# Low-rank products added to the base weights once per batch, in a kernel of attention, low-rank feed-forward and routed experts

## The reference, cut to what matters

```python
y = einsum(x, weight[id]) + bias[id]                       # cond
Q, K, V = y @ W_Q, y @ W_K, y @ W_V                        # 16 heads of 16
x1 = x + softmax(causal(Q K^T / 4)) V @ W_o
hid = relu(x1 @ wi^T + 2*(x1 @ common_wi_a^T) @ common_wi_b^T + 2*(x1 @ Wa_i[id]^T) @ Wb_i[id]^T)
h = hid @ wo^T + 2*(hid @ common_wo_a^T) @ common_wo_b^T + 2*(hid @ Wa_o[id]^T) @ Wb_o[id]^T   # F = 1024, ranks 16 + 16
out = x1 + top2 of 8 experts(h), three dense layers 256-512-512-256 with gelu, weighted by the softmax gate
```

## Time and profile before

| what | value |
|---|---|
| median of 3 runs | 1477.07 us (1468.75 to 1480.15) |
| the profiled execution | 1473.53 us, its span 1471.8 us |
| mean granted PE clock | 0.94 |
| busy: PE, DVE, ACT, POOL | 1299.8, 814.7, 682.5, 515.0 us |

### The profile page before, as it was taken

How to read it: one execution, slowest core, us unless ns; L and a number is a source line. 1 busy time by engine, 2 the same in 40 slices (tenths; PEclk the granted TensorE clock), 3 DMA queues, 4 the chain that set the end, 5 groups by cost and what they waited for, 6 DMA issues and landing times.

```text
span 1471.8 us, 26713 instructions
## 1 busy us (share of the span) xinstructions
PE 1299.8 (88%) x8313; PEld 974.7 (66%) x8314; DVE 814.7 (55%) x1753; ACT 682.5 (46%) x1301; POOL 515.0 (35%) x809
## 2 busy tenths in 40 slices
PE   5878989988988988989989885459899999999997
PEld 3436656656656656656666554448788888888886
DVE  4626646646646646556556433745455555555553
ACT  4654654655655655655655630023333333333332
POOL 0332332332332432432332420324354444544442
PEclk9579999999999999999999978569999999999998
DMA  5112223222232132132132223733525224242220
GB/s 176 44 48 89 83 77 116 79 85 96 80 123 87 64 122 82 65 123 87 55 113 79 80 86 129 292 137 73 217 43 155 36 43 141 52 148 38 38 43 11
DMA packets 50765, 137.54 MB, mean 93 GB/s; under 512 B 10658, under 2 KB 29730, under 8 KB 49026
## 3 DMA queue, kind: packets, MB, share of 16 engines
q0 software_dynamic: 28992, 68.35, 16.4%
q1 hardware_dynamic: 21698, 68.18, 12.8%
HBM read 86.03 MB, written 51.38 MB: 93 GB/s over the span
## 4 chain that ended last, share of the span: by engine, by line
PE 71%; DVE 11%; ACT 8%; DMA 3%; issue 3%; POOL 3%; SPq 0%; POOLq 0%; DVEq 0%; ACTq 0%
PE bank L691 65%; PE bank L973 4%; DVE nmax L1359 4%; ACT q_sb L1160 3%; ACT probs_t L1153 2%; PE bank L965 1%; DVE hid_low L1286 1%; DMA xg<-hrows,gid 1%; POOL w_rest L1617 1%; ACT ot_sb L1169 1%; DMA out<-y_sb,sid 1%; POOL wsplit L1621 1%; PE bank L893 1%; DVE mm_sb L1366 1%; ACT sums L1170 1%
## 5 line engine op out<-in xcount | busy, mean ns | idle before, releaser
L1359 DVE TENSOR_REDUCE nmax<-bank 128x1 f32<-128x512 f32 (+3 forms) x512 | 221.4, 485 | 120.7 <-PE bank L691 120.4
L1153 ACT ACTIVATE probs_t<-bank 128x512 f32<-128x512 f32 (+1 forms) x384 | 181.1, 524 | 119.8 <-PE bank L691 119.3
L1193 ACT ACTIVATE g<-z 128x512 f32<-128x512 f32 x142 | 89.8, 632 | 280.6 <-DVE z L1555 280.6
L1603 POOL TENSOR_SCALAR_AFFINE_SELECT probs_t<-probs_t 128x256 f32<-128x256 f32 x256 | 97.8, 406 | 336.3 <-ACT probs_t L1153 336.1
L691 PE MATMUL bank<-wst,g1t_high 128*128 x568 | 185.7, 408 | 0.9 <-DVE g1t_low L1543 0.9
L1665 POOL DMA_INDIRECT out<-y_sb,sid x71 | 114.4, 1611 | 152.1 <-DVE y_sb L1576 69.0
L1617 POOL TENSOR_TENSOR w_rest<-w_rest,w_high 128x512 f32<-128x512 f32 x64 | 82.0, 1282 | 173.5 <-ACT w_high L1039 173.5
L1555 DVE TENSOR_TENSOR z<-bank,b_sb 128x512 f32<-128x512 f32 x142 | 98.2, 692 | 73.3 <-PE bank L691 62.6
L691 PEld LDWEIGHTS bank<-wst,g1t_high 128*128 128x128 f32 x568 | 102.6, 191 | 20.6 <-issue 1.1
L691 PE MATMUL bank<-wst,g1t_low 128*128 x284 | 113.1, 398 | 0.0
L691 PE MATMUL bank<-wst,g2t_high 128*128 x568 | 108.4, 291 | 1.5 <-DVE g2t_low L1543 1.5
(11 more groups left out here) (223 smaller groups left out, 2879.4 us busy)
## 6 DMA issues: line engine op xcount, KB each, us to landing
wst<-wsplit SPq DMA_DIRECT2D x8, 4096.0 KB, 12.5
w_rest<-in_w_all POOLq DMA_DIRECT2D x64, 256.0 KB, 2.9
wsplit<-w_high POOLq DMA_DIRECT2D x64, 256.0 KB, 2.3
wsplit<-w_rest POOLq DMA_DIRECT2D x64, 256.0 KB, 2.5
hrows<-h_sb SPq DMA_DIRECT2D x8, 528.0 KB, 4.0
x_in<-in_xT SPq DMA_DIRECT2D x8, 512.0 KB, 3.7
wb_raw<-in_lora_wb SPq DMA_DIRECT2D x8, 512.0 KB, 3.5
x1t<-in_xT SPq DMA_DIRECT2D x8, 512.0 KB, 4.3
```

The lines of the kernel that those rows point to most:

```text
L1153: taken(nc.scalar.activation(probs_t[:, (2 * g + half) % PT_SLOTS, S * u:S * u + width], at(n, rd)[:, 0:width], ACT.Exp), n, rd)
L1193: nc.scalar.activation(g[:, :], z[:, :], ACT.Gelu).then_inc(s_g, 1)
L1359: ins = V.tensor_reduce(nmax[:, g % 2, half, i:i + 1], at(n, rd)[:, cols], AX.X, ALU.max, negate=True)
L1603: ins = nc.gpsimd.affine_select(diag, diag, [[0, 2], [1, P]], ALU.is_ge, 0.0, base=0, channel_multiplier=-1)
```

## The change

For each batch the low-rank products are multiplied out and added to the base weights: `wi_b = wi + 2 A B`. Eight merges do it, each one PSUM bank of 128x512: four for wi (one matmul of 512 columns each), four for wo (two of 256). DVE adds a merge to a piece of base weights that SP loads anew each time into one buffer, `w_stage` (256 KB, loaded when the merge before has been added); ACT copies the sum to the high part two steps after the merge, DVE subtracts to the low part three steps after. `low_i`, `low_o` and the extra matmuls of `hid` and `h` go. The factors are loaded as four 128-row tensors in two loads (at and wb, ao and bo) and split at other steps. `h` starts in step 5, `next` stands in steps 25 to 28, `gate` in step 32. In the opening q and k of the second chunk and the first eight strips now come ahead of `x1t`. `at` is renamed `at_bank` throughout; `CASTS_AFTER`, `CAST_STEPS` and `CAST_EARLY` are unchanged.

```diff
-FILLERS = ([(("hid", j), k) for j in range(HID_EARLY, KF) for k in range(KD)] +
-           [(("x1", t2), 0) for t2 in range(TB // 2)] + [(("low_o", 0), piece) for piece in range(LOW_PIECES)] +
-           [(("h", t), piece) for t in range(TB) for piece in range(H_PIECES)] +
-           [(("next", 0), 0), (("next", 0), 1), (("ht", 0), 0), (("next", 1), 0), (("ht", 1), 0), (("next", 1), 1),
-            (("gate", 0), 0), (("softmax", 0), 0)])
-FILL_COUNTS = [2] * 5 + [1] * 7 + [0] + [1] * 5 + [0, 1, 0, 1, 1, 1, 0] + [2] * 5 + [0, 1, 0, 1]
-LORA_STEPS = {29: (0, 1), 30: (1, 2), 31: (2, 3), 32: (3, 4), 33: (4, 6)}
-LOW_STEPS = {30: (0, 1), 32: (1, 2), 33: (2, 4)}
+MID = ([[item] for item in H_ITEMS[:7]] + [[]] + [[item] for item in H_ITEMS[7:12]] + [[]] +
+       [[item] for item in H_ITEMS[12:]] + [[], []])
+TAIL = [[(("next", 0), 0)], [(("next", 0), 1)], [(("next", 1), 0)], [(("next", 1), 1)], [(("ht", 0), 0)], [],
+        [(("ht", 1), 0)], [(("gate", 0), 0)], [(("softmax", 0), 0)]]
+FILL = HID_STEPS + [X1_STEP] + MID + TAIL
+MERGE_STEPS = {4: 0, 7: 1, 10: 2, 14: 3, 25: 4, 27: 5, 29: 6, 31: 7}
+LORA_O_STEPS, LORA_I_STEPS, LORA_FIRST_STEPS = {9: 0, 11: 1}, {19: 0, 21: 1}, {0: 0, 2: 1}
...
-    order += [("q", 0), ("k", 0), ("x1t", 0), ("x1t", 1), ("q", 1), ("k", 1), ("v", 0)]
-    order += quads[0] + [("low_i", 0)] + quads[1] + [("hid", 0), ("v", 1)] + quads[2] + [("hid", 1)] + quads[3]
+    order += [("q", 0), ("k", 0), ("q", 1), ("k", 1)] + quads[0] + quads[1] + [("x1t", 0), ("x1t", 1), ("v", 0)] + [("hid", 0), ("v", 1)] + quads[2] + [("hid", 1)] + quads[3]
...
+            def stage_after(rd, n):
+
+                drained(sp, ("merge", n), rd)
+                stage((n + 1) % MERGES)
...
+                if b is not None and p is not None:
+                    filled(sp, ("merge", MERGES - 1), Round(p))
+                    load_lora_o(expert_of(b))
...
+                if b is not None:
+                    for n in range(MERGES // 2 - 1):
+                        stage_after(rd, n)
+                    if rd.leads:
+                        filled(sp, ("merge", MERGES // 2 - 1), rd)
+                        load_lora_i(e_next)
+                    for n in range(MERGES // 2 - 1, MERGES if rd.leads else MERGES - 1):
+                        stage_after(rd, n)
...
-                elif what == "low_i":
+                elif what == "merge":
                     vacant(pe, n, rd)
...
+                    if m < MERGES // 2:
+                        k, cols = m % KD, slice(m // KD * S, (m // KD + 1) * S)
+                        ins = mm(dst()[:, :], at[:, k * P:(k + 1) * P], wb[:, cols], start=True, stop=True)
+                    else:
+                        for u in range(2):
+                            j = 2 * (m - MERGES // 2) + u
+                            ins = mm(dst()[:, u * D:(u + 1) * D], ao[:, j * P:(j + 1) * P], bo[:, :], start=True, stop=True)
...
-                    ins = mm(dst()[:, :], wb[:, m * P:(m + 1) * P], low_i[:, :], start=False, stop=True)
...
-                    ins = mm(dst()[:, 0:D], low_o[:, m * P:(m + 1) * P], bo[:, :], start=False, stop=True)
...
+            def merge_high(rd, n):
+
+                drained(act, n, rd)
+                high, _, raw, _ = merged(n[1])
+                nc.scalar.copy(high, raw).then_inc(s_merge_high, 1)
...
+                    for n in merges(rd, step - 2):
+                        merge_high(rd, n)
...
+            def merge_low(b, n):
+
+                high, low, raw, _ = merged(n[1])
+                dve.wait_ge(s_merge_high, MERGES * b + n[1] + 1)
+                V.tensor_tensor(low, raw, high.bitcast(F32), ALU.subtract).then_inc(s_merge_low, 1)
...
+                elif what == "merge":
+                    dve.wait_ge(s_stage, 16 * (MERGES * b + m + 1))
+                    if p is not None:
+                        filled(dve, ("hid", 3) if m < 2 else ("hid", KF - 1) if m < MERGES // 2 else ("h", TB - 1), rd)
+                    filled(dve, n, rd)
+                    ins = V.scalar_tensor_tensor(merged(m)[2], at_bank(n, rd)[:, :], 2.0, w_stage[:, :], ALU.mult, ALU.add)
```

More of the change, by code:

```diff
@@ L40 @@
 COPIES = 4
-LORA_LOADS, LORA_HIGHS, LORA_LOWS = 4, 6, 4
-BASE_PIECES = 8
+LORA_PARTS = 4
+MERGES = 8
 NE = 8
@@ L113, with fillers_at @@
 CAST_EARLY = {1: 7}
[L116 to L121, removed]
+def fillers_at(step, attends, feeds, leads):
+    merges = [merge(MERGE_STEPS[step])] if attends and step in MERGE_STEPS else []
+    return [(name, piece) for name, piece in FILL[step] if (leads if name[0] == "next" else feeds)] + merges
 def opening(attends, feeds):
@@ L167, in psum_plan @@
             take(("nr", scale), "score")
-        for name, piece in fillers_at(step, feeds, leads):
+        for name, piece in fillers_at(step, attends, feeds, leads):
             if piece == 0 and name[0] != "softmax":
@@ L173, in psum_plan @@
     return plan, uses
-assert len(FILL_COUNTS) == STEPS and len(FILLERS) == sum(FILL_COUNTS)
+assert len(FILL) == STEPS
 class Round:
@@ L302, in build_kernel @@
         bo = sb("bo", [COPIES * RANK, D], F32R, part_a)
[L303 to L305 removed]
+        w_stage = sb("w_stage", [P, S], F32, part_a)
         with ExitStack() as shared:
@@ L504, in taken, with merged, merges @@
             ins.then_inc(free[rd.plan[name][0]], 1)
[L506 to L512, removed]
+        def merged(n):
+            if n < MERGES // 2:
+                k, cols = n % KD, slice(n // KD * S, (n // KD + 1) * S)
+                return wi_high[:, k, cols], wi_low[:, k, cols], wi_raw[:, k, cols], wi_t[:, k, cols]
+            rows = slice(2 * (n - MERGES // 2), 2 * (n - MERGES // 2) + 2)
+            return (*(w[:, rows, :].rearrange("p j d -> p (j d)") for w in (wf_high, wf_low, wf_raw)), wo_t[:, rows, :])
+        def merges(rd, step):
+            return [name for name, _ in rd.fillers(step) if name[0] == "merge"] if 0 <= step < STEPS else []
+        lora_i = ((wb_raw, wb, F, 4), (at_raw, at, D, 3))
+        lora_o = ((ao_raw, ao, F, 3), (bo_raw, bo, D, 4))
         def query_tiles(u):
@@ L587, in _ @@
             x1s = [("x1", t2) for t2 in range(TB // 2)]
[L589 to L609, removed]
-                    else:
[L611 to L616, removed]
-                if rd.p is not None:
-                    wait_for(rd, free, x1s, v_x1)
-                    if rd.b is not None:
-                        load_res(rd.b)
-                    sp.dma_start(out[bass.ds(p, 1), :, :].rearrange("o (t p) d -> p (o t) d", p=P),
-                                 x1_sb[:, :, :]).then_inc(s_x1out, 16)
-                    if rd.b is not None:
-                        wait_for(rd, full, hs, v_h)
-                        sp.wait_ge(s_x1out, 16 * (rd.p + 1) + 1)
-                        load_lora(e)
-                    sp.wait_ge(s_hdone, v_hdone)
-                    sp.sem_inc(s_tick, 1)
-                    sp.dma_start(hrows[bass.ds(p * S, S), :].rearrange("(t p) d -> p t d", p=P),
@@ L649, in _ @@
                 turn(Round(b))
-            turn(Round(B - 1), last=True)
+            turn(Round(B - 1))
             turn(Round(B))
@@ L1053, in take @@
                     filled(act, n, rd)
-                    nc.scalar.copy(parts[:, m, 0 if what == "q" else 2, :], at(n, rd)[:, :]).then_inc(s_hi, 1)
+                    nc.scalar.copy(parts[:, m, 0 if what == "q" else 2, :], at_bank(n, rd)[:, :]).then_inc(s_hi, 1)
                     return
@@ L1334, in turn @@
                         take(rd, n)
-                    if before is not None and n != ("low_i", 0):
+                    if before is not None and n != ("hid", 0):
                         low_part(rd, before)
```

306 lines of the change are left out of this document (146 added, 160 removed).

## The result

| | before | after |
|---|---|---|
| median of 4 runs each, same chip | 1478.06 us (1468.75 to 1480.15) | 1543.10 us (1538.00 to 1547.76) |
| ratio, 95% interval | | 1.0457 (1.0411 to 1.0503) |
| span of the profiled execution | 1471.8 us | 1546.0 us |
| mean granted PE clock | 0.940 | 0.911 |

What follows compares the result with a forecast made beforehand. It took TensorE's matmuls as the bound, with in-order DVE and ACT waits eating the saving; -3 + 6 x (3.2 + 2.0 - 1.7) + (3.2 + 2.0 - 0.5) - 3 = +19.7 us, forecast 1495, range 1450 to 1515.

Steps and rivals of the forecast that it cites:

- rival C: Slower: the gap in the opening drops the clock in each of 7 rounds, 1.5 us each, to 1506; chance 0.15.
- The loop of casts: Opening: cast 6 can't start until 8.96 us after cast 5, so ACT stands 6 us and TensorE idles 5.0 us.
- the opening: Start of each round 1 to 7: +3.2 us, its 1.9 us of saved matmuls included; bounds 0 and 4.7.
- The tail: Last ten steps of a round: cast 3 comes 1.2 us sooner, another 0.8 saved, -1.7 us in all; bounds -3 and +1.
- From the gate product of round 7 to that of round 8: Last round: h starts where low_o did, -4.2 us, with 1.2 back for a slow clock: -3.
- The wait for h(1)'s bank: Score steps 8 to 9: h(1) waits for DVE to free h(0)'s bank, 1.5 us lost per round.
- Bank 7: Score steps: h(0), h(1), h(2) share one bank; waits of 1.5 us at h(1), 1.3 at h(2), 2.8 per round.
- The splits and merges: Score steps: factor splits and merge pieces on DVE and ACT, overruns in steps 9 and 10, 0.5 us per round.
- round 0: First round: loses eight base splits and their load wait, shorter tail, merges at low clock: -3 us; bounds -6 and +3.
- A: Faster: TensorE alone decides, casts and banks are absorbed, 41 us saved, 1436; chance 0.14.
- B: No change: the cast wait costs 3.2 us per round, but TensorE makes up the bank waits, 1470; chance 0.24.
- D: Slower: four low halves per round in the score steps collide with GpSimd's subtract, 2.6 us per round, 1513; chance 0.05.

Runs made afterwards that it cites:

- e7: Changed kernel with 18 extra matmuls, results overwritten, at the head of hid(1) in the opening, where TensorE stood waiting; 1521.09 us, ratio 1.0278.
- e1: Changed kernel with weight casts 5 and 6 moved behind the strips ks 3 and ks 7, cast 7 one step later; 1480.56 us, ratio 1.0044.
- e4: Kernel before with only the new order of the opening, low_i right ahead of hid(0), no merges, casts not moved; 1509.49 us, ratio 1.0223.
- e5: Changed kernel with e1's moved casts, merges 1 to 3 on the bank of the h behind them, and merge 3 one step later; 1478.25 us, ratio 1.0009.
- e9: e5 with factor splits moved to steps 16, 18, 23 and 25 and the last three pieces of h to steps 21 to 23; 1464.97 us, ratio 0.9943.
- e8: e5 with each merge's DVE add, ACT cast and DVE subtract cut from 512 to 8 columns in rounds 1 to 7; 1466.66 us, ratio 0.9949.
- e6: e5 with factor splits moved: lora_o to steps 19 and 21, lora_i to 26 and 28; 1472.67 us, ratio 0.9978.
- e10: e9 with the ring of score banks begun at bank 1 instead of 0; 1450.28 us, ratio 0.9809.
- e12: e10 with 8 extra 256-column matmuls at merge 4 and 5 at merge 5 in rounds 1 to 7, results overwritten; 1442.53 us, ratio 0.9773.
- e11: Kernel before with only the ring of score banks begun at bank 2; 1467.67 us, ratio 0.9947.

## Why the prediction was wrong in size

**The step that failed** is the clock: the sum put the half clock behind the gap at nothing and named it only as rival C, at 1.5 us per round. The runs show 3.7 us per round for it, and slow tails besides, which neither the sum nor C had.

**Held.** The loop of casts and where ACT and PE stand: cast 5 at 13.0 (13.5), cast 6 at 21.9 (22.5), PE idle 4.43 (5.0). At full clock (e7, five rounds) the opening costs 30.4 - 27.2 = 3.2 us more than before, which is the forecast, though e7's round 4 alone would give 2.2. That the casts make this wait, e1 shows: with them moved the 33.1 us of PE are gone. e4 shows that the new order with the old casts slows the kernel without any merge, but with a third of that wait. The tail: six at full clock would be 22.0 each, -10.6 in all against -10.2; behind the last maxima cast 3 comes 1.9 us sooner (10.5 instead of 12.4) and the last value product 1.3 (15.4 instead of 16.7), where 1.2 was forecast. From the gate product of round 7 to that of round 8: 52.8 to 48.0 us, -4.8 against -3. The wait for h(1)'s bank: 1.35 against 1.5.

**Failed: the clock, which I made a rival and priced too low.** Rival C ("the gap in the opening drops the clock in each of 7 rounds, 1.5 us each") got 0.15, and its gap was certain by my own walk. It should have been part of the forecast. It was also mis-sized. By e7 the half clock costs 2.4 us in an opening and 59.1 - 57.8 = 1.3 in the steps behind it: (2.4 + 1.3) x 7 = 26 us. I had priced six matmuls; the granted clock stayed at half for the 7 us of the row above, and in five of seven rounds fell again at the head of the steps. Two tails at 5.7 us are another 11, and round 7's tail, from the last maxima to the gate product, took 23.6 us where it had 19.8 and should have lost 0.5:

```profile
830.10:849.80 19.70, 14.51 (x122) 8.70 (x120) 2.33 (x6) 11.57 (x22) 6.95 (x15) 0.87 0.33 117
903.80:927.40 23.60, 15.01 (x102) 7.77 (x103) 7.03 (x11) 10.76 (x22) 7.44 (x15) 0.71 0.28 97
```

(before, then after). That makes 26 + 11 + 4 = 41 of the 54 us by which the span missed the sum. Against C I had held that 306 to 327 kept 0.97 with 4 us idle. But those 4 us came in waits of at most 2.0, while the new gap is 4.4 in one piece. For the tails this doesn't serve: no wait of PE in the changed kernel's tails of rounds 1 to 6 is longer than 1.6 us, and two of them fell to half clock even so. The Trainium skill ("TensorE: Matmul & The Clock Gate", What's actually happening) was what I cited for C, and the openings of this trace agree with it: half rate after the gap, full rate again behind dense work.

**Failed: two terms of the steps.** At full clock the steps grew by 57.8 - 54.6 = 3.2 us per round, forecast 2.0. Bank 7 was worth 1.6, not 2.8. The second wait was too large, since h(2) starts later than I read off the old order. The splits and merges, put at 0.5, were worth 1.4 (e5 to e9, steps 3 to 23) and 0.8 (e8). I had looked for overruns step by step but not at the one place where a 1.28 us split follows the reciprocals. With the -1.3 of matmuls this makes 2.5 of the 3.2.

**Missed: round 0**, +2.4 against -3. Its steps took 60.2 us instead of 56.5, its tail 23.2 instead of 27.8; no run takes this apart. One profile of a kernel says little here: e5 and e8 have the same round 0, and it ends at 117.1 and 120.3 us.

**The rivals.** A and B fell with the first row of PE's waits (B's terms give 1472, not the 1470 written there). D (DVE against GpSimd) is there, but smaller: in most rounds the `ao` split took 1.71 us where `wb` always took 1.28, and two of four wi subtracts 0.87 to 0.89 where the others took 0.68:

```profile
L1235 DVE SCALAR_TENSOR_TENSOR ao<-lora_top,marks_sb,ao_raw x8: 1277/1712/1717, 56.6 to 872.1; 128x1024 fp32r<-128x1024 f32 x8
L1242 DVE TENSOR_TENSOR wi_low<-wi_raw,wi_high x32: 678/778/1330, 49.5 to 890.0; 128x512 fp32r<-128x512 f32 x32
```

(ns, shortest, median, longest). That is some 0.8 us of DVE per round against D's 2.6. A GpSimd operation overlaps each of these in the trace, but also some that were not slowed, so the cause stays open.

**Still open:** what sets off the 14 us of half clock in a tail (of the six tails of rounds 1 to 6, two in the changed kernel, one each in e6, e7, e8 and e10, none in the others), with one profile to a kernel; and how much of e12's lead over before is the merging, since the kernel before got only the bank repair (e11), not its own pass over idle times, and its casts were never moved.

## What to carry to other kernels

When a list of products is reordered, the other in-order lists that were tuned against it (here ACT's casts, which wait for a transfer loop of about 9 us) must move with it; three numbers were worth 62 of 65 us here. In this kernel a gap of 4 to 5 us in a dense stretch of matmuls cost its length and some 3.7 us more for the half clock after it; such a term belongs in the sum. An idle TensorE with nothing useful to do may be given work it throws away (some 20 us in e7). And a saving that equals the count (opening -2.0 for 1.9 in e1) can be two other terms that cancel. With casts, h banks and splits moved (e9) the merging is no slower than the kernel before (ratio 0.9943), so it was the schedule that cost the 65 us.

## What the runs showed of the hardware

The clock fell in every kernel, the ones before the change and the repaired ones too, and not only behind long gaps: 14 us at 0.51 stand in a tail whose longest wait is 1.6 us, while an opening of e7 kept 1.00 through a wait of 3.11 us. In e5 the steps were shorter and four tails 1.7 us longer, at 0.93, which ate most of the gain; whether the one caused the other was not tried. And matmuls whose results are overwritten shortened a run (e7, 1543 to 1521 us), which no count of work would show.
